# Key-value products of linear attention: one head per matmul, 64 key columns by 65 value columns, instead of a pair of heads per matmul

## The reference, cut to what matters

```python
xn = _layernorm(x, axis=-1)
# _L0_mix_ref(xn[None], w_qkv, w_o): b = 1, s = 625, h = 16 heads, d = 64
qkv = (x @ w_qkv).reshape(b, s, 3, h, d)
q, k, v = (qkv[:, :, 0], qkv[:, :, 1], qkv[:, :, 2])
q = jax.nn.elu(q) + 1.0
k = jax.nn.elu(k) + 1.0
kv = jnp.einsum('bnhd,bnhf->bhdf', k, v)      # per head: 64 x 64, summed over the 625 nodes
k_sum = k.sum(axis=1)                         # per head: 64
numerator = jnp.einsum('bnhd,bhdf->bnhf', q, kv)
denominator = jnp.einsum('bnhd,bhd->bnh', q, k_sum)[..., None] + 1e-06
attn = (numerator / denominator).reshape(b, s, dm)
return attn @ w_o
```

## Time and profile before

| | |
|---|---|
| median of 3 runs | 474.67 us (471.54 to 475.95) |
| profiled execution, its own time | 472.26 us |
| its span, first to last instruction | 470.3 us |
| mean granted TensorE clock | 0.996 of full speed |
| PE (matmul) busy | 448.4 us, 95% of the span, 2627 records |
| PEld (weight load) busy | 387.3 us, 82% |
| DVE / ACT / POOL busy | 342.4 / 190.3 / 138.8 us |

### The profile page before, as it was taken

The page is one execution under the profiler, slowest core; times in us unless marked ns, Lnnn a source line. Parts: engine busy times, 40 slices in busy tenths (PEclk is TensorE's granted clock), DMA queues, the critical chain, the costliest instruction groups (busy, mean ns, idle before and its releaser), DMA issues.

```text
span 470.3 us, 8191 instructions
## 1 busy us (share of the span) xinstructions
PE 448.4 (95%) x2627; PEld 387.3 (82%) x2627; DVE 342.4 (73%) x905; ACT 190.3 (40%) x337; POOL 138.8 (30%) x105
## 2 busy tenths in 40 slices
PE   7889999989999899999999999999999999999897
PEld 5779998767788787779888877799999988888665
DVE  6999995998569778983057799744564548788873
ACT  2566562215173565445144744334443222111262
POOL 2421123443431522222232222226776200023400
PEclk9989999999999999999999999999999999999999
DMA  8722240222221311111121111025655001130024
GB/s 213 233 91 89 91 136 0 74 84 67 67 67 47 89 47 45 46 45 41 28 67 58 52 46 43 26 86 158 188 172 179 24 0 47 45 90 0 1 89 131
DMA packets 19206, 36.45 MB, mean 77 GB/s; under 512 B 2593, under 2 KB 2843, under 8 KB 19054
## 3 DMA queue, kind: packets, MB, share of 16 engines
q1 hardware_dynamic: 19179, 36.11, 26.3%
HBM read 33.54 MB, written 2.56 MB: 77 GB/s over the span
## 4 chain that ended last, share of the span: by engine, by line
PE 66%; DVE 21%; issue 7%; ACT 3%; DMA 1%; DVEq 1%; SPq 0%; ACTq 0%
PE ps L988 15%; PE ps L989 15%; PE ps L990 15%; PE ps L1015 9%; PE ps L1240 4%; PE ps L1078 2%; PE ps L1110 2%; PE ps L1127 2%; DVE onehot_src L588 2%; DVE exp_a L751 2%; DVE onehot_dst L586 2%; DVE score L732 2%; DVE junk L678 1%; DVE k_sb L721 1%; DVE packed L642 1%
## 5 line engine op out<-in xcount | busy, mean ns | idle before, releaser
L304 POOL TENSOR_TENSOR w_lo<-w_raw,w_hi 128x512 fp32r<-128x512 f32 x52 | 74.1, 1428 | 180.0 <-ACT w_hi L344 180.0
L988 PE MATMUL ps<-w_hi,act_hi 128*125 128x512 f32 x240 | 96.7, 403 | 2.2 <-ACT tmp L417 2.2
L989 PE MATMUL ps<-w_lo,act_hi 128*125 128x512 f32 x240 | 94.6, 394 | 0.0
L990 PE MATMUL ps<-w_hi,act_lo 128*125 128x512 f32 x240 | 94.5, 394 | 0.0
L1015 PE MATMUL ps<-onehot_src,onehot_dst 125*125 125x314 bf16 x400 | 61.5, 315 | 5.4 <-DVE onehot_src L588 5.4
L1015 PEld LDWEIGHTS ps<-onehot_src,onehot_dst 125*125 125x125 bf16 x400 | 56.2, 145 | 10.3 <-DVE onehot_src L588 6.5
L344 ACT ACTIVATE w_hi<-w_raw 128x512 fp32r<-128x512 f32 x52 | 32.8, 633 | 74.3 <-PE ps L990 72.9
L988 PEld LDWEIGHTS ps<-w_hi,act_hi 128*125 128x125 f32 x240 | 44.5, 185 | 12.8 <-ACT tmp L417 2.6
L990 PEld LDWEIGHTS ps<-w_hi,act_lo 128*125 128x125 f32 x240 | 44.5, 185 | 11.3
L989 PEld LDWEIGHTS ps<-w_lo,act_hi 128*125 128x125 f32 x240 | 44.5, 185 | 9.9
L988 PE MATMUL ps<-act_hi,w_hi 128*128 128x312 f32 (+1 forms) x128 | 39.7, 310 | 0.0
(11 more groups left out here) (151 smaller groups left out, 880.0 us busy)
## 6 DMA issues: line engine op xcount, KB each, us to landing
w_raw<-in_weights SPq DMA_DIRECT2D x80, 256.0 KB, 2.7
f_raw<-in_ffn_weights SPq DMA_DIRECT2D x32, 256.0 KB, 2.7
x_sb<-in_x SPq DMA_DIRECT2D x5, 448.0 KB
out<-x_sb SPq DMA_DIRECT2D x9, 224.0 KB
alr<-in_a_lr SPq DMA_DIRECT2D x1, 896.0 KB
bias_sb<-in_bias SPq DMA_DIRECT2D x1, 448.0 KB
x_sb<-in_x SPq DMA_DIRECT2D x5, 52.0 KB
out<-x_sb SPq DMA_DIRECT2D x9, 26.0 KB
```

Of the source, the lines that this page charges most:

```text
L304: pool.tensor_tensor(w_lo[:, s, :], w_raw[:, s, :], w_hi[:, s, :].bitcast(f32), ALU.subtract).then_inc(w_ready, 1)
L988: pe.matmul(dst, a[0], b[0], start=first, stop=False)
L989: pe.matmul(dst, a[0], b[1], start=False, stop=False)
L990: return pe.matmul(dst, a[1], b[0], start=False, stop=last)
```

## The change

The values get a column of ones behind each head's 64 columns, not behind each pair's 128. A pair's matmul becomes two: head 0's 64 key columns by its 65 value columns, written to PSUM partitions 0 to 63, then head 1's, written to partitions 64 to 127, at the same PSUM columns. The copies out of PSUM take the same blocks from their new places. Numbers of waits and signals, the order of tiles and banks, and all transfers stay.

```diff
-        v_sb = at("v_sb", [P, NT, HP, PAIR + 1], f32, AREA + 51200)
+        v_sb = at("v_sb", [P, NT, HP, 2, DK + 1], f32, AREA + 51200)
...
-                            act.activation(v_sb[:, nt, :, 0:PAIR],
-                                           ps[:P, nt, :].rearrange("p (r f) -> p r f", f=PAIR),
+                            act.activation(v_sb[:, nt, :, :, 0:DK],
+                                           ps[:P, nt, :].rearrange("p (r h f) -> p r h f", h=2, f=DK),
                                            ACT.Copy).then_inc(bank_free, 1)
...
-            dve.memset(v_sb[:, :, :, PAIR:PAIR + 1], 1.0).then_inc(ones_v, 1)
+            dve.memset(v_sb[:, :, :, :, DK:DK + 1], 1.0).then_inc(ones_v, 1)
...
                         rws = slice(h * DK, (h + 1) * DK)
-                        src = ps[rws, 5 + b, :2 * (PAIR + 1)].rearrange("p (r f) -> p r f", f=PAIR + 1)
+                        src = ps[rws, 5 + b, :2 * (DK + 1)].rearrange("p (r f) -> p r f", f=DK + 1)
                         dst = kv_blocks[rws, ds(j * HP + 2 * b, 2), :]
-                        dve.tensor_copy(dst[:, :, h * DK:(h + 1) * DK], src[:, :, h * DK:(h + 1) * DK]).then_inc(kv_free, 1)
-                        dve.tensor_copy(dst[:, :, PAIR + h:PAIR + h + 1], src[:, :, PAIR:PAIR + 1]).then_inc(kv_free, 1)
+                        dve.tensor_copy(dst[:, :, h * DK:(h + 1) * DK], src[:, :, :DK]).then_inc(kv_free, 1)
+                        dve.tensor_copy(dst[:, :, PAIR + h:PAIR + h + 1], src[:, :, DK:DK + 1]).then_inc(kv_free, 1)
...
                         for nt in range(NT):
-                            last = pe.matmul(ps[:, 5 + b, r * (PAIR + 1):(r + 1) * (PAIR + 1)],
-                                             k_sb[:, nt, pr_ * PAIR:(pr_ + 1) * PAIR], v_sb[:, nt, pr_, :],
-                                             start=nt == 0, stop=nt == NT - 1)
+                            for h in range(2):
+                                col = pr_ * PAIR + h * DK
+                                last = pe.matmul(ps[h * DK:(h + 1) * DK, 5 + b, r * (DK + 1):(r + 1) * (DK + 1)],
+                                                 k_sb[:, nt, col:col + DK], v_sb[:, nt, pr_, h, :],
+                                                 start=nt == 0, stop=nt == NT - 1)
                     last.then_inc(kv_done, 1)
```

## The result

The changed kernel takes 469.08 us in the median of 20 runs (467.31 to 472.98), the kernel before 472.36 (20 runs, 471.38 to 477.91). The ratio is 0.993 with a 95% interval of [0.9908, 0.9953]: 3.3 us faster, clear of noise, within 1%. Forecast were 3.8 us saved and 469.8 us.

The account below looks back on a forecast made before the run. TensorE's own pace was taken to bound the two line-1110 blocks: 8.76 us becomes 4.38 + 0.6 = 4.98, 3.8 saved, so 469.8 us from a level of 473.6. The range was 467.3 to 476.5 us, rival 3 left out.

Parts of the forecast that it names:

- Both on the chain, nothing hides them: Both line-1110 matmul blocks, 8.76 us in all, lie whole on the last chain; each us saved there passes on in full.
- The price of a record, lower end: Line-1110 blocks: the halves load and stream beside each other, 2.19 us a block instead of 4.38, 4.38 saved in all.
- Halved, each is about 55 ns: Line-1110 records: weight load and column stream, about 109 ns each, both shrink to about 55 ns at half width.
- the order of the records: Two records per head in turn let neighbours of different heads run together; given in support of the lower end.
- Change of division, 0.15 each: Switching between whole and halved array before and behind each block: four changes, 0.15 us each, 0.6 in all.
- Value copies, ones, copies out of PSUM at nothing: ScalarE's value copies (0.98 us of cover), the memset of ones and the copies out of PSUM (L803, L804): no cost.
- Rival 1, turns: Line-1110 blocks: halves take turns, 80 records of 55 ns a block, nothing gained, 474.2 us; chance 0.29.
- Rival 2, a floor at 40 ns: Line-1110 blocks: halves overlap but records start no faster than 40 ns, block 3.2 us, 471.8 us; chance 0.13.
- nothing in the trace goes below 52 ns: Starts of narrow records (line 1038) come 52 ns apart at the least, so pairs 27 ns apart on average weren't shown.
- Rival 3, loads without cover: Line-1110 blocks: loads can't run during the other half's matmul, 109.5 ns a record, 8.8 us lost, 483.0 us; chance 0.10.
- The level: Base of the forecast: mean 473.6 us of four readings of the kernel before, 4.4 us from lowest to highest.

Follow-up runs that it names:

- experiment 7: Changed kernel, GpSimd's bias adds held, each pair's head loop outside its tile loop, both heads in one array half: block 4.81 us, end 473.93 us.
- experiments 10 and 11: Four whole-array matmuls added a block, bias adds held, in the changed kernel (471.74 us) and the kernel before (475.94): +0.89 and +0.43 us from last aggregation to next line.
- experiment 3: Changed kernel with the bias transfer issued early and its first three bias adds held until VectorE's L916 of tile 2: 471.82 us (10 runs).
- experiment 11: Kernel before with GpSimd's bias adds held and four whole-array matmuls of 2 columns added a block, one ahead of each pair: 475.94 us (one run).
- held kernel before: Kernel before with GpSimd's bias adds held until VectorE finished tile 2's second normalisation: 471.50 us (12 runs).

## Why the prediction was right

*Both on the chain, nothing hides them.* Held: 1.78 us read at one block, 3.58 for both in the profiles and 3.96 in the end time once the race is out.

*The price of a record, lower end (2.19 us a block).* Right in mechanism, too low in size: 2.48 measured. The overlap itself is whole. The records start in pairs, 7 and 52 ns apart in turn, 29.5 ns on average, and in one half alone (experiment 7) they start 59 ns apart, twice that. What was too low is the line before it, "Halved, each is about 55 ns": a half-width record takes 59. That makes 0.17 of the 0.29 us, 0.05 of it because the second pair comes 0.1 us after the first. The other 0.12 is the step from the last record to the next line, 0.15 us where 0.03 was reckoned. The reason that I gave, the order of the records, was not needed: four in a row for one half do nearly as well. What sets the 59 ns stays open in part. It is not the load: a quarter loads half as much and its records come round every 57 ns. It may be the 65 moving columns, or a floor near 58 ns, which is also the distance of L1038's records with 2 moving columns, behind their first; no run separates the two.

*Change of division, 0.15 each.* At most 0.08 to 0.11 by experiments 10 and 11; the block's late start is 0.09. This term was too high, the one before it too low, and their sum, 2.49 a block, meets the 2.48 + 0.09 measured to 0.1 us. That closeness is partly luck.

*Value copies, ones, copies out of PSUM at nothing.* Held. PE does not wait at either block.

*Rival 1, turns.* Excluded: taking turns looks like experiment 7, 4.81 us. *Rival 2, a floor at 40 ns.* Excluded: 31 ns here, 14 with quarters. The premise that nothing in the trace goes below 52 ns holds for means only: the five records of L1038 start 28 ns apart at first and 58 after that. *Rival 3, loads without cover.* Excluded: 80 loads of 138 ns start within 2.3 us. Even in one half a record takes 60 ns, less than load and stream in a row (110). The rule that I quoted for this rival from the Trainium skill (TensorE: Matmul & The Clock Gate, Part 3, The mechanism: loads overlap matmuls in flight only where the row group differs) is not what this case shows: both heads use the same rows, and loads and matmuls overlap. What TensorEngine Tiling (Array Packing) in the Trainium skill says under Key Properties, that tiles load and multiply in parallel, the trace bears out.

*The level.* I took the spread of the runs (4.4 us) as noise around 473.6. Part of it has causes: lost races, shown for the changed kernel, and stretches at the low clock of about 1.6 us each. For the kernel before the lower group, 472.0, was the right base; with it the same sum gives 468.2, and the lower group of the changed kernel is at 468.0. My 469.8 came out close to the median of 469.08 because that median is drawn up by 8 upper readings of 20. That is luck: the saving was right, the base 1.6 too high, and the changed kernel's lost races made up for most of it.

## What to carry to other kernels

If two products each need at most half of the array's columns, give them different halves and alternate them at least every few matmuls: each pair then takes the time of one half-width matmul (59 ns for two records here). It pays only where TensorE's own pace is the bound. Here load and stream both shrank. From halves to quarters the load alone shrinks, and a block gets no shorter. Narrowing without a partner at work costs time (4.81 us against 4.38). And when runs of one kernel fall in groups some us apart, compare the profile's durations of the same small operations and the granted clock stretch by stretch before calling it noise; to judge a change of 2 us a block, compare the block and not the end of a single run.

## What was not expected of the hardware

- While GpSimd adds two f32 tiles in SBUF, some of VectorE's operations on SBUF last until an add is over, however small they are: L569 and L925, one column with two SBUF inputs each, 2.27 and 2.30 us where 0.16 and 0.22 are normal; L947, 5 columns with one input, 1.52 where 0.23 is; L812, 512 columns with one input, 1.99 where 0.48 is (in the kernel before). Others on SBUF alone are not stretched beside the same adds: the reciprocals of L827 (0.13 to 0.17 us), L943 on one column (0.15), the statistics of L894 (0.41 and 0.43) and the reduction of L876 (0.67). Nor are those that read PSUM. The Trainium skill, Advanced Engine Details and Errata, VectorE Performance Modes, says that VectorE's second SBUF port is shared with GpSimd and that instructions of GpSimd and two-port instructions of VectorE block each other. The trace agrees that some are blocked and others not; in which mode each ran, no row says.
- In both profiles with the stall (the changed kernel and experiment 3) it shows on TensorE twice: as a wait (2.06 us), and as a granted clock of 0.58 and 0.75 over the next 5.5 us, with matmuls 0.43 us apart in place of 0.23, the lower of its two levels (1.2 for 2.4 GHz) for a part of that stretch. In no profile without the stall does the clock fall there.
- Stretches at the lower level come elsewhere too, in one execution and not in the next of nearly the same program, and cost about 1.6 us each where TensorE sets the pace (1.6 from 28 to 41 us in the kernel before, 1.57 around 107 us in experiment 11, 1.65 late in it). TensorE had idled ahead of the late one (busy 1.84 us of 4.00 in 446.00:450.00 of experiment 11), but in the held kernel before, busy 2.24 us of 4.00 in 442.00:446.00, the clock stayed at 1.00 behind it.
- f32 records in quarters of the array start 14 ns apart on average (7 ns within a group of four, then mostly 34 to 37); the shortest mean distance read in the kernel before was 52 ns, and its f32 records of L1110 came every 109.5 ns.
